# Value products one step later, and the key/value products split around the query products, in a two-layer cross-attention kernel

## The chip, the cores and the metric

One Trainium2 chip, one of its cores. The metric is the device time of one execution in microseconds (us), lower is better; the kernel before was timed three times, and its median is 1316.86 us (1316.17 to 1316.87).

## What is computed

Two layers of a gated cross-attention model on x (8 batches of 128 tokens, 512 wide) and a context of the same size:

```python
x = x + tanh(g_xattn[0]) * xattn0(layernorm(x), ctx, mask, ...)   # 32 query heads, 8 key/value heads, 128 wide
x = x + tanh(g_ffn[0])   * ffn0(layernorm(x), ...)                # gated, block-quantised weights and inputs
x = x + tanh(g_xattn[1]) * xattn1(layernorm(x), ctx, mask, ...)
x = x + tanh(g_ffn[1])   * ffn1(layernorm(x), ...)                # int4 weights, permuted inputs, bias
```

In an attention, q and k are normalised over each head (x * rsqrt(mean(x^2) + eps)), the softmax runs over 128 context positions in fp32, and four query heads share one key/value head.

## The kernel before, in words

**Units and steps.** A unit is one group (one key/value head with its four query heads) of one batch: 8 groups x 8 batches x 2 layers = 128 units. The kernel is a software pipeline of steps; step n works on four units at once. For unit n it makes keys and values (kv), queries (q), their normalisation and transposes; for unit n-1 the scores and the softmax; for unit n-2 the transposed probabilities and the value products; for unit n-3 the output products, which are added into x. Each engine has one function `step`, whose order of statements is the order of its queue; the engines meet only at semaphores.

**Products.** An fp32 product is made of three products of rounded halves (`hi` times `hi`, `hi` times `lo`, `lo` times `hi`), each over four k-tiles: `three_products` issues 12 matmuls, 512 wide for q and output, 256 wide for kv. The values take three matmuls. ScalarE (ACT) makes the `hi` half, VectorE (DVE) the `lo` half by subtraction. So `oT_hi`/`oT_lo` are halves of the attention output of unit n-3, both made from the PSUM bank `psPO`, and `pT_hi`/`pT_lo` those of the transposed probabilities.

**Steps 75 to 123.** Here (`by_dma`) the probabilities are not transposed on TensorE (PE). DVE writes them as two 16-bit planes (`probs_planes`), SyncE (SP) turns them with one DMA transpose (`turn_probs`), and DVE (`place_lower`, line 1027) and ACT (line 786) put the halves together in `p_whole`; ACT copies `pT_hi` from it (line 790) and DVE subtracts `pT_lo` (line 1032). In such a step PE's queue is: 12 kv, 12 q, 4 scores (8 records, as fp32 runs in two passes), 12 output, one transpose of k (`transposed_k`), 3 values, four transposes of q (`transposed_q`). `output()` waits for `o_lod`, the semaphore of `oT_lo`, ahead of its first product; `values()` waits for `pt_lod`, that of `pT_lo`; `transposed_k` waits for `kn_done`, the normalised keys.

**The other engines in such a step.** ACT: `oT_hi` (line 739), up to two or three pieces of weights rounded to `w_hi` (line 730), the square of k (748), `v_hi` (751), the four squares of q (769), `p_whole` and `pT_hi` (786, 790), the scaled `kn` (719), four exponentials (711), `qT` (836). DVE: inverse row sums, scaled probabilities, the planes, `oT_lo` (1085), `v_lo` (1102), `place_lower` (1027), masked scores (1138), maximum (1010), `pT_lo` (1032), scaled q (`qn`, 1040), `kT` (1164), the addition into x (1176). GpSimd (POOL): `w_lo` of the pieces (551), then the two small operations (576, 580) that turn the sums of squares into `rstd`, of which `kn` and `qn` are made.

**Around them.** Steps 0 to 47 are the first layer with the quantisation of feed-forward weights, steps 48 to 87 a written-out zone with the feed-forward of the first layer, steps 88 to 119 a loop of eight steps a turn (PE's own loop begins at step 80), and steps 120 on the last group and the second feed-forward. From step 124 on the probabilities are transposed on PE again.

Of the kernel before, what the change touches and what calls it, by code (L numbers as in the profile page):

```python
# [15 lines left out]
P = 128  # L16
# [80 lines left out]
def step_of(group, b):  # L97
# [6 lines left out]
              32: ((E + 1, 6), (E + 1, 7)), 33: ((E + 1, 8), (E + 1, 9), (E + 2, 0)), 34: ((E + 2, 1), (E + 2, 2)),  # L104
              35: ((E + 2, 3),), 36: ((E + 2, 4), (E + 2, 5)), 37: ((E + 2, 6),), 38: ((E + 2, 7), (E + 2, 8)),
# [51 lines left out]
def flamingo_kernel(nc, x, ctxT, mask, g_xattn, g_ffn, norms, wq, wkv, wo, ffn_w,  # L157
                    packedT, scalesT, perm, bias, w4_rows, out):
    top = ExitStack()
    with top:  # L160
# [211 lines left out]

        def turned_by_pe(n):

            return n - 1 - (DMA1 - DMA0 if isinstance(n, int) and n >= DMA1 else 0)
# [161 lines left out]
        def _(pool):  # L537
# [72 lines left out]
            def step(n, b, kind, j, q=None):  # L610
# [13 lines left out]
                if kind in (ZONE, PLAIN) and not calm(n, kind):  # L624
                    split_lower(split_pieces(n, b, kind, j))
# [46 lines left out]
        def _(act):  # L672
# [58 lines left out]

            def step(n, b, kind, j, q=None):
                t = Tiles(n, kind)
                exp_late = calm(n, kind) or (kind == FIRST and b == BATCHES - 1)
                if has(n, 3):

                    act.wait_ge(pv_ps, n - 2)
                    wait(act, y_ps, n - 3)
                    nc.scalar.activation(oT_hi[:, :], psPO[:, :], ACT.Copy).then_inc(o_hid, 1)
                if calm(n, kind) or (kind == ZONE and n == FFN0):  # L740
                    softmax_exp(n - 1)
                if kind in (ZONE, PLAIN) and not calm(n, kind):
                    split_upper(split_pieces(n, b, kind, j))
                if has(n, 0):

                    act.wait_ge(kv_ps, n + 1)
                    wait(act, rs_done, n)
                    nc.scalar.activation(kn[:, 0:P // 2].bitcast(BF16), kv_bank(n, kind)[:, 0:P], ACT.Square, scale=SCALE, accum_out=sumsq[:, REP:REP + 1])

                    wait(act, pv_ps, n - 3)  # L750
                    nc.scalar.activation(v_hi[:, b % 4, :], kv_bank(n, kind)[:, P:2 * P], ACT.Copy).then_inc(v_hid, 1)
                split_upper(late_pieces(n, kind))
# [12 lines left out]
                if has(n, 0):  # L765

                    act.wait_ge(q_ps, n + 1)
                    for h in range(REP):
                        last = nc.scalar.activation(squares[:, h // 2, (b + 1) % 4, h % 2, :], q_bank(n, kind)[:, h * P:(h + 1) * P], ACT.Square, scale=SCALE,  # L769
                                                    accum_out=sumsq[:, h:h + 1])  # L770
                    last.then_inc(sq_done, 1)
# [10 lines left out]
                if has(n, 2) and by_dma(n, kind):  # L782

                    act.wait_ge(pv_ps, n - 2)
                    act.wait_ge(planes_turned, (n - DMA0 + 1) * 16)
                    nc.scalar.activation(halves(p_whole[:, :])[:, :, 1], p_turned[:, 0:KT, :].rearrange("p k t -> p (k t)"),
                                         ACT.Copy).then_inc(upper_placed, 1)
                    act.wait_ge(upper_placed, n - DMA0 + 2)
                    act.wait_ge(lower_placed, n - DMA0 + 2)
                    nc.scalar.activation(pT_hi[:, :], p_whole[:, :], ACT.Copy).then_inc(pt_hid, 1)  # L790
# [36 lines left out]
                if has(n, 0):  # L827
# [8 lines left out]
                    nc.scalar.activation(qT[:, :], psSQ[:, :], ACT.Copy).then_inc(qT_sb, 1)  # L836
                if has(n, 1) and (t.next is not None or t.down is not None):
                    softmax_exp(n)
# [34 lines left out]
        def _(dve):  # L873
# [156 lines left out]
            def probs_lower(n, kind=None):  # L1030
                dve.wait_ge(pt_hid, n - 1)
                nc.vector.tensor_tensor(pT_lo[:, :], (p_whole if by_dma(n, kind) else psPO)[:, :], pT_hi[:, :].bitcast(FP32),
                                        ALU.subtract).then_inc(pt_lod, 1)
# [27 lines left out]
            def step(n, b, kind, j, q=None):  # L1061
# [5 lines left out]
                if has(n, 2):  # L1067

                    if not calm(n, kind):
                        row_inverse(n)  # L1070
                if by_dma(n, kind):
                    scaled_probs(n)
                    probs_planes(n)
                if q is not None and 0 < b <= QSTEPS:
# [7 lines left out]
                if has(n, 3):  # L1082

                    dve.wait_ge(o_hid, n - 2)
                    nc.vector.tensor_tensor(oT_lo[:, :], psPO[:, :], oT_hi[:, :].bitcast(FP32),
                                            ALU.subtract).then_inc(o_lod, 1)
# [3 lines left out]
                if t.last is not None:  # L1090
                    dve.wait_ge(x_acc, LAST0 + t.last + 1)
                    moments(NORM["last", t.last], t.last)
# [4 lines left out]
                if has(n, 2) and not t.active and not by_dma(n, kind):  # L1097
# [8 lines left out]
                if kind == ZONE and 0 <= n - INT4_0 < INT4_PARTS:  # L1106
                    int4_weights(n - INT4_0)
                for k in gathered(n, kind):

                    dve.wait_ge(wp_hid, k + 1)  # L1110
                    nc.vector.tensor_tensor(wp_lo[:, k, :], w4_turned[:, k, :], wp_hi[:, k, :].bitcast(FP32),
                                            ALU.subtract).then_inc(wp_lod, 1)
# [3 lines left out]
                if t.last is not None:  # L1116
                    wait(dve, xT_ps, 2 * BATCHES + t.last if t.last else 0)
                    normalise(NORM["last", t.last], t.last, f_s[:, :])
# [10 lines left out]
                if by_dma(n, kind):  # L1129
                    place_lower(n)  # L1130
# [12 lines left out]
                if by_dma(n, kind):  # L1143
                    probs_lower(n, kind)
                if has(n, 2) and (t.gate is not None or calm(n, kind)):
                    probs_lower(n, kind)
                if has(n, 0) and kind != FIRST and t.down is None:
                    scaled_q(n, kind, t)
                if has(n, 2) and qn_first(n, kind, t) and not calm(n, kind):
                    probs_lower(n, kind)  # L1150
# [4 lines left out]
                if has(n, 2) and t.gate is None and not qn_first(n, kind, t) and not by_dma(n, kind):  # L1155
                    probs_lower(n, kind)
# [13 lines left out]
                if has(n, 3):  # L1170
# [6 lines left out]
                                                   ALU.mult, ALU.add).then_inc(x_acc, 1)  # L1177
                if t.gate is not None:
# [107 lines left out]
        def _(pe):  # L1286
# [59 lines left out]
            def step(n, b, kind, j, q=None):  # L1346
# [22 lines left out]
                def output():  # L1369
                    pe.wait_ge(o_lod, n - 2)  # L1370
                    wait(pe, x_acc, n - 3)
                    if batch_of(n, 3, b) == 0:
                        pe.wait_ge(whole_w, group_of(n, 3, b, j) + 1)
                    three_products(psY[:, :], lambda a, h: (oT_hi, oT_lo)[a][:, h * P:(h + 1) * P],
                                   lambda a, h: weights(3, WO0 + h * D, D)[a]).then_inc(y_ps, 1)
# [13 lines left out]
                def values():  # L1389
                    pe.wait_ge(pt_lod, n - 1)  # L1390
                    if by_dma(n, kind):
                        pe.wait_ge(o_lod, n - 2)
                    slot = (b - 2) % 4
# [26 lines left out]
                if has(n, 0) and kind != FIRST:  # L1420
                    batch = batch_of(n, 0, b)

                    if kind != FIRST and batch == 0:
                        pe.wait_ge(qkv_split, group_of(n, 0, b, j))
                    wait(pe, kT_sb, n)
                    tok = slice(batch * P, (batch + 1) * P)
                    three_products(psKV[:, 0:2 * P], lambda a, k: (ctx_hi, ctx_lo)[a][:, batch, k * P:(k + 1) * P],
# [161 lines left out]
```

## Time and profile before

| what | value |
|---|---|
| median of three runs | 1316.86 us |
| the profiled execution | 1317.38 us, of it span 1315.6 us |
| PE busy | 1301.6 us, 99% |
| weight loads of PE (PEld) busy | 1102.0 us, 84% |
| DVE / ACT / POOL busy | 1002.2 / 866.9 / 621.4 us |
| granted TensorE clock | 1.000 over the whole span |
| HBM | 46 GB/s over the span |

The span runs from the first to the last instruction; the rest of the execution, 1.8 us, lies outside it. The ends of matmuls are modelled, so PE's busy share overstates its use: the distances between the starts of matmuls tell more than the share. Two layers of 128 steps fill the span, so one step of steps 75 to 123 takes about 9 us.

### The profile page before, as it was taken

What the parts mean: (1) busy time and instruction counts of PE and PEld (TensorE: products, weight loads), DVE (VectorE), ACT (ScalarE), POOL (GpSimd) and SP (SyncE); (2) the same over time, 40 slices, a digit from 0 to 9 for tenths busy, and PEclk for the clock granted to TensorE, in tenths of its full rate; (3) what the DMA queues carried; (4) which work ended last, traced back from release to release, by engine and by line L of the source; (5) the groups of instructions that cost most, each with busy time, mean ns of one, the idle gap of its engine ahead of it and who ended that gap; (6) DMA issues with size and microseconds to landing.
All of it is one profiled execution on the core that took longest, in us unless ns stands there. A gap on an engine that the chain in (4) does not pass through costs nothing.

```text
span 1315.6 us, 25535 instructions
## 1 busy us (share of the span) xinstructions
PE 1301.6 (99%) x7493; PEld 1102.0 (84%) x7493; DVE 1002.2 (76%) x2106; ACT 866.9 (66%) x3356; POOL 621.4 (47%) x683
## 2 busy tenths in 40 slices
PE   8999999999999999999999999999999999999999
PEld 7888888888888888877777788888888888888887
DVE  6878788787878788688888858777667677676756
ACT  5767667676767776645566456777767777676651
POOL 2546566565646566446677533532323323232232
PEclk9999999999999999999999999999999999999999
DMA  7011110111121011020301013623222122321001
GB/s 298 1 56 57 63 56 20 66 50 68 50 68 50 24 68 47 13 64 20 103 20 48 20 48 89 161 65 73 64 66 70 36 71 61 80 56 33 17 9 57
DMA packets 87338, 78.29 MB, mean 60 GB/s; under 512 B 70881, under 2 KB 75873, under 8 KB 83169
## 3 DMA queue, kind: packets, MB, share of 16 engines
q1 hardware_dynamic: 70272, 71.91, 18.6%
q10 hardware_dynamic: 16672, 4.46, 1.6%
q0 software_dynamic: 320, 1.05, 0.2%
q8 instruction: 33, 0.54, 0.2%
q14 instruction: 41, 0.33, 0.1%
HBM read 57.48 MB, written 3.15 MB: 46 GB/s over the span
## 4 chain that ended last, share of the span: by engine, by line
PE 84%; DVE 5%; issue 5%; DMA 2%; POOL 2%; ACT 1%; ACTq 0%; POOLq 0%; DVEq 0%; SPq 0%
PE bank L1298 60%; PE bank L1364 7%; PE bank L1290 7%; PE bank L1395 6%; PE bank L1326 2%; DMA p_turned<-p_planes 1%; PE bank L1381 1%; PE bank L1479 1%; POOL rstd L580 1%; DMA f_iqT<-f_iq 1%; DVE probs L1138 1%; ACT squares L769 0%; DMA ctx_raw<-in_ctxT 0%; DVE f_q L975 0%; DVE amax L968 0%
## 5 line engine op out<-in xcount | busy, mean ns | idle before, releaser
L551 POOL TENSOR_TENSOR w_lo<-w_raw,w_hi (+1 forms) x150 | 192.7, 1301 | 163.9 <-ACT w_hi L730 163.9
L769 ACT ACTIVATE squares<-bank 128x128 bf16<-128x128 f32 x512 | 134.4, 278 | 184.6 <-PE bank L1298 184.5
L711 ACT ACTIVATE probs<-probs,negmax 128x128 f32<-128x128 f32 x512 | 198.2, 391 | 7.0 <-DVE negmax L1010 4.5
L576 POOL TENSOR_TENSOR meansq<-sumsq,scalars 128x5 f32<-128x5 f32 x128 | 27.5, 215 | 352.5 <-ACT squares L769 352.5
L580 POOL TENSOR_TENSOR rstd<-meansq,scalars 128x5 f32<-128x5 f32 x128 | 152.9, 1194 | 10.7 <-POOL meansq L576 1.1
L1298 PE MATMUL bank<-w_hi,oT_hi 128*128 (+1 forms) x512 | 150.9, 416 | 0.0
L1298 PE MATMUL bank<-w_hi,xT_hi 128*128 (+1 forms) x512 | 140.1, 395 | 0.0
L1298 PE MATMUL bank<-w_lo,xT_hi 128*128 (+1 forms) x512 | 138.1, 390 | 0.3
L1364 PEld LDWEIGHTS bank<-kT,qT 128*128 128x128 f32 x1024 | 131.7, 191 | 7.7
L1298 PE MATMUL bank<-w_hi,oT_lo 128*128 (+1 forms) x512 | 138.0, 391 | 0.0
L1298 PE MATMUL bank<-w_lo,oT_hi 128*128 (+1 forms) x512 | 137.6, 390 | 0.0
L1298 PE MATMUL bank<-w_hi,xT_lo 128*128 (+1 forms) x512 | 136.9, 389 | 0.0
L1364 PE MATMUL bank<-kT,qT 128*128 128x128 f32 x1024 | 134.8, 274 | 0.0
L1138 DVE SCALAR_TENSOR_TENSOR probs<-bank,mask_sb 128x512 f32<-128x512 f32 x127 | 87.5, 689 | 58.3 <-PE bank L1364 40.5
L1298 PEld LDWEIGHTS bank<-w_lo,xT_hi 128*128 128x128 f32 x512 | 96.1, 188 | 22.7 <-DVE w_lo L904 1.4
L1298 PEld LDWEIGHTS bank<-w_lo,oT_hi 128*128 128x128 f32 x512 | 96.1, 188 | 21.6
L1298 PEld LDWEIGHTS bank<-w_hi,oT_lo 128*128 128x128 f32 x512 | 96.1, 188 | 21.2
L1298 PEld LDWEIGHTS bank<-w_hi,xT_lo 128*128 128x128 f32 x512 | 96.1, 188 | 19.9
L769 ACT ACTIVATION_READ_ACCUMULATOR squares<-bank 128x1 f32 x512 | 106.5, 208 | 0.0
L1298 PEld LDWEIGHTS bank<-w_hi,xT_hi 128*128 128x128 f32 x512 | 88.0, 189 | 11.8
L1298 PEld LDWEIGHTS bank<-w_hi,oT_hi 128*128 128x128 f32 x512 | 87.5, 189 | 12.4
L711 ACT ACTIVATION_READ_ACCUMULATOR probs<-probs,negmax 128x1 f32 x512 | 96.9, 189 | 0.0
(129 smaller groups left out, 3000.2 us busy)
## 6 DMA issues: line engine op xcount, KB each, us to landing
w_raw<-in_wq SPq DMA_DIRECT2D x16, 1024.0 KB, 4.8
w_raw<-in_wo SPq DMA_DIRECT2D x16, 1024.0 KB, 9.6
w_raw<-in_wkv SPq DMA_DIRECT2D x16, 512.0 KB, 5.6
fw_raw<-in_ffn_w SPq DMA_DIRECT2D x36, 192.0 KB, 2.3
x_sb<-in_x SPq DMA_DIRECT2D x7, 256.0 KB, 10.4
ctx_raw<-in_ctxT SPq DMA_DIRECT2D x7, 256.0 KB, 9.8
fw_raw<-in_ffn_w SPq DMA_DIRECT2D x7, 256.0 KB, 2.6
out<-x_sb SPq DMA_DIRECT2D x7, 256.0 KB, 2.0
```

The costliest lines, as they stand in the source:

```text
L551: last = nc.gpsimd.tensor_tensor(lo, raw, hi.bitcast(FP32), ALU.subtract)
L576: nc.gpsimd.tensor_tensor(meansq[:, :], sumsq[:, :], eps_sb[:, :], ALU.add).then_inc(ms_done, 1)
L580: nc.gpsimd.tensor_tensor(rstd[:, :], meansq[:, :], minus_half[:, :], ALU.pow).then_inc(rs_done, 1)
L711: last = nc.scalar.activation(probs[:, h * P:(h + 1) * P], probs[:, h * P:(h + 1) * P], ACT.Exp, bias=negmax[:, h:h + 1], accum_out=rowsum ...
L769: last = nc.scalar.activation(squares[:, h // 2, (b + 1) % 4, h % 2, :], q_bank(n, kind)[:, h * P:(h + 1) * P], ACT.Square, scale=SCALE, a ...
L1138: nc.vector.scalar_tensor_tensor(heads(probs[:, :]), heads(psSQ[:, :]), SCALE, mask_sb[:, :].unsqueeze(1).to_broadcast([P, REP, P]), ALU.m ...
L1290: last = nc.tensor.transpose(dst[:, k * P:(k + 1) * P], src[:, k * P:(k + 1) * P], m)
L1298: last = nc.tensor.matmul(dst, left(a, k), right(b, k), start=(n == 0), stop=(n == len(terms) - 1))
L1326: last = nc.tensor.matmul(ps[:, 0:width], f_xqT[:, k, :], wT[:, col:col + width], start=(k == 0), stop=(k == KT - 1))
L1364: last = nc.tensor.matmul(psSQ[:, h * P:(h + 1) * P], qT[:, h * P:(h + 1) * P], kT[:, :], start=True, stop=True)
L1381: nc.tensor.transpose(kv_bank(n, kind)[:, 2 * P:3 * P], kn[:, :], ident[:, :]).then_inc(kt_ps, 1)
L1395: last = nc.tensor.matmul(psPO[:, :], v[:, slot, :], p[:, :], start=(k == 0), stop=(k == 2))
```

## The change

It concerns steps 76 to 124 (`values_late`), all but the first of the steps with a DMA transpose and the one behind them.

- PE: four of the 12 kv products, then the 12 q products, then the three value products of unit n-3 (one step later than before), then the other eight kv products, scores, the first eight output products, the transpose of k, the last four output products, the four transposes of q.
- ACT: the squares of q come first (their unused output goes to `qn`'s memory), then `oT_hi`, then the square of k (which now signals `sq_done`), `v_hi`, the pieces of `w_hi`; the halves `p_whole` and `pT_hi` move to the end of the step, behind `qT`, also in step 75.
- DVE: `pT_lo` of the step before stands between the scaled probabilities and the planes, `oT_lo` behind the planes, `place_lower` at the end of the step.
- POOL: `rstd` comes ahead of the step's `w_lo`.
- The pieces of weights in steps 81 to 83 are dealt out two a step; one-off work of the zone is moved on DVE; in step 124 the moments and the normalisation of the first batch of the second feed-forward come earlier on DVE.

```diff
+        def values_late(n, kind):
+            return kind == PLAIN or (isinstance(n, int) and DMA0 < n <= DMA1)
@@ POOL
-                if kind in (ZONE, PLAIN) and not calm(n, kind):
+                if kind in (ZONE, PLAIN) and not calm(n, kind) and not values_late(n, kind):
                     split_lower(split_pieces(n, b, kind, j))
...
+                if values_late(n, kind):
+                    split_lower(split_pieces(n, b, kind, j))
@@ ACT
+            def q_squares(n, b, kind):
+                act.wait_ge(q_ps, n + 1)
+                for h in range(REP):
+                    dump = (qn[:, h * P // 2:(h + 1) * P // 2].bitcast(BF16) if values_late(n, kind)
+                            else squares[:, h // 2, (b + 1) % 4, h % 2, :])
+                    last = nc.scalar.activation(dump, q_bank(n, kind)[:, h * P:(h + 1) * P], ACT.Square, scale=SCALE,
+                                                accum_out=sumsq[:, h:h + 1])
+                return last
+            def output_upper(n):
+                act.wait_ge(pv_ps, n - 2)
+                wait(act, y_ps, n - 3)
+                nc.scalar.activation(oT_hi[:, :], psPO[:, :], ACT.Copy).then_inc(o_hid, 1)
...
                 if has(n, 0):
+                    if values_late(n, kind):
+                        q_squares(n, b, kind)
+                        output_upper(n)
                     act.wait_ge(kv_ps, n + 1)
...
+                if values_late(n, kind):
+                    split_upper(split_pieces(n, b, kind, j))
...
+                if has(n, 2) and by_dma(n, kind):
+                    if not values_late(n, kind):
+                        act.wait_ge(pv_ps, n - 2)
+                    act.wait_ge(planes_turned, (n - DMA0 + 1) * 16)
+                    nc.scalar.activation(halves(p_whole[:, :])[:, :, 1], ...).then_inc(upper_placed, 1)
+                    act.wait_ge(upper_placed, n - DMA0 + 2)
+                    act.wait_ge(lower_placed, n - DMA0 + 2)
+                    nc.scalar.activation(pT_hi[:, :], p_whole[:, :], ACT.Copy).then_inc(pt_hid, 1)
@@ DVE
+            def whole_lower(n):
+                dve.wait_ge(pt_hid, n - 2)
+                nc.vector.tensor_tensor(pT_lo[:, :], p_whole[:, :], pT_hi[:, :].bitcast(FP32),
+                                        ALU.subtract).then_inc(pt_lod, 1)
...
+                if by_dma(n, kind) or t.last == 0:
+                    scaled_probs(n)
+                if values_late(n, kind):
+                    whole_lower(n)
                 if by_dma(n, kind):
-                    scaled_probs(n)
                     probs_planes(n)
...
+                if values_late(n, kind):
+                    output_lower(n)
...
+                if by_dma(n, kind):
+                    place_lower(n)
@@ PE
-                    three_products(psY[:, :], ...).then_inc(y_ps, 1)
+                    for part in (slice(0, 2 * KT), slice(2 * KT, 3 * KT)):
+                        last = three_products(psY[:, :], ..., part)
+                        if values_late(n, kind) and has(n, 0) and part.start == 0:
+                            transposed_k()
+                    last.then_inc(y_ps, 1)
...
+                    if values_late(n, kind):
+                        wait(pe, kT_sb, n)
+                        keys_values(slice(0, KT))
+                        queries()
+                        values(3)
+                        keys_values(slice(KT, 3 * KT)).then_inc(kv_ps, 1)
```

## Rows read from the trace of the kernel before

**Rows 1.** Timeline, PE, one step: start us, us, engine, line, operation, count.
```profile
1018.28 0.72 PE L1298 MATMUL bank<-w_hi,ctx_hi 128*128 x4
1018.84 0.64 PE L1298 MATMUL bank<-w_lo,ctx_hi 128*128 x4
...
1019.80 1.09 PE L1298 MATMUL bank<-w_hi,xT_hi 128*128 x4
...
1022.55 1.05 PE L1364 MATMUL bank<-kT,qT 128*128 128x128 f32 x8
1023.36 1.17 PE L1298 MATMUL bank<-w_hi,oT_hi 128*128 x4
...
1026.18 0.28 PE L1381 MATMUL bank<-ident,kn 128*128 128x128 f32 x1
1026.21 0.48 PE L1395 MATMUL bank<-pT_hi,v_hi 128*128 128x512 f32 x1
...
1027.35 0.71 PE L1298 MATMUL bank<-w_hi,ctx_hi 128*128 x4
```

**Rows 2.** Timeline, PE, the scores of steps 75, 76, 123 and 124.
```profile
790.32 1.05 PE L1364 MATMUL bank<-kT,qT 128*128 128x128 f32 x8
...
800.60 1.05 PE L1364 MATMUL bank<-kT,qT 128*128 128x128 f32 x8
...
1231.05 1.05 PE L1364 MATMUL bank<-kT,qT 128*128 128x128 f32 x8
...
1241.65 0.61 PE L1364 MATMUL bank<-kT,qT 128*128 128x128 f32 x4
```

**Rows 3.** Waits of weight loads, 789 to 1232 us: total us, times, longest.
```profile
PEld bank L1381 <- ACT kn L719: 4.3, 5, 1.5
```

**Rows 4.** Timeline, the longest wait: DMA transpose issued, and its reader.
```profile
835.50 1.23 SPq L486 DMA_TRANSPOSE p_turned<-p_planes  x1
...
841.05 0.78 ACT L786 ACTIVATE p_whole<-p_turned 128x512 uint16<-128x512 uint16 x1 [1.82 <-DMA p_turned<-p_planes]
```

**Rows 5.** Timeline, the other engines in the step of rows 1.
```profile
1018.62 0.60 ACT L836 ACTIVATE qT<-bank 128x512 f32<-128x512 f32 x1 [0.34 <-PE bank L1290]
...
1019.12 0.59 ACT L739 ACTIVATE oT_hi<-bank 128x512 fp32r<-128x512 f32 x1
...
1019.96 0.68 DVE L1085 TENSOR_TENSOR oT_lo<-bank,oT_hi 128x512 fp32r<-128x512 f32 x1
...
1020.15 1.23 SPq L486 DMA_TRANSPOSE p_turned<-p_planes  x1
...
1022.75 0.28 ACT L769 ACTIVATE squares<-bank 128x128 bf16<-128x128 f32 x1 [1.58 <-PE bank L1298]
...
1023.20 0.46 DVE L1027 COPY p_whole<-p_turned 128x512 uint16<-128x512 uint16 x1 [1.70 <-DMA p_turned<-p_planes]
...
1023.76 0.80 ACT L786 ACTIVATE p_whole<-p_turned 128x512 uint16<-128x512 uint16 x1
...
1024.24 1.17 POOL L580 TENSOR_TENSOR rstd<-meansq,scalars 128x5 f32<-128x5 f32 x1
...
1024.59 0.63 ACT L790 ACTIVATE pT_hi<-p_whole 128x512 fp32r<-128x512 f32 x1
...
1025.25 0.69 DVE L1032 TENSOR_TENSOR pT_lo<-p_whole,pT_hi 128x512 fp32r<-128x512 f32 x1 [0.20 <-ACT pT_hi L790]
1025.44 0.37 ACT L719 ACTIVATE kn<-bank,rstd 128x128 f32<-128x128 f32 x1 [0.22 <-POOL rstd L580]
```

**Rows 6.** Timeline, a weight load that waited for DVE.
```profile
762.72 0.68 DVE L1032 TENSOR_TENSOR pT_lo<-bank,pT_hi 128x512 fp32r<-128x512 f32 x1
...
763.45 0.19 PEld L1395 LDWEIGHTS bank<-pT_hi,v_hi 128*128 128x128 f32 x1
```

**Rows 7.** Timeline, DVE beside POOL's `w_lo` in one step.
```profile
807.41 2.72 POOL L551 TENSOR_TENSOR w_lo<-w_raw,w_hi 128x512 fp32r<-128x512 f32 x2 [3.96 <-ACT w_hi L730]
...
808.91 1.51 DVE L1052 TENSOR_SCALAR nibble_i<-packed_sb 128x512 int32<-128x512 int32 x1
```

More of the change, by code:

```diff
@@ L764, in step @@
                     hidden_turned(0, t.down)
[L765 to L771, printed above, removed]
+                if has(n, 0) and not values_late(n, kind):
+                    q_squares(n, b, kind).then_inc(sq_done, 1)
                 if t.first is not None:
@@ L1028, in place_lower, with last_normalised, output_lower, probs_lower @@
                                       ).then_inc(lower_placed, 1)
-            def probs_lower(n, kind=None):
+            def last_normalised(i):
+                wait(dve, xT_ps, 2 * BATCHES + i if i else 0)
+                normalise(NORM["last", i], i, f_s[:, :])
+            def whole_lower(n):
+                dve.wait_ge(pt_hid, n - 2)
+                nc.vector.tensor_tensor(pT_lo[:, :], p_whole[:, :], pT_hi[:, :].bitcast(FP32),
+                                        ALU.subtract).then_inc(pt_lod, 1)
+            def output_lower(n):
+                dve.wait_ge(o_hid, n - 2)
+                nc.vector.tensor_tensor(oT_lo[:, :], psPO[:, :], oT_hi[:, :].bitcast(FP32),
+                                        ALU.subtract).then_inc(o_lod, 1)
+            def probs_lower(n):
                 dve.wait_ge(pt_hid, n - 1)
-                nc.vector.tensor_tensor(pT_lo[:, :], (p_whole if by_dma(n, kind) else psPO)[:, :], pT_hi[:, :].bitcast(FP32),
+                nc.vector.tensor_tensor(pT_lo[:, :], psPO[:, :], pT_hi[:, :].bitcast(FP32),
                                         ALU.subtract).then_inc(pt_lod, 1)
@@ L1081, in step @@
                     nc.vector.scalar_tensor_tensor(xb, psC[:, :], down_gate[:, :], xb, ALU.mult, ALU.add).then_inc(d_acc, 1)
[L1082 to L1086, printed above, removed]
+                if has(n, 3) and not values_late(n, kind):
+                    output_lower(n)
                 if t.acc is not None:
@@ L1096, in step @@
                     row_inverse(n)
-                if has(n, 2) and not t.active and not by_dma(n, kind):
+                if has(n, 2) and not t.active and not by_dma(n, kind) and t.last != 0:
                     scaled_probs(n)
@@ L1105, in step @@
                         ctx_lower(t.first)
-                if kind == ZONE and 0 <= n - INT4_0 < INT4_PARTS:
+                if kind == ZONE and 0 <= n - INT4_0 < INT4_PARTS and not values_late(n, kind):
                     int4_weights(n - INT4_0)
[L1108 to L1112, printed above, removed]
                 if t.first is not None:
@@ L1115, in step @@
                     normalise(t.first, t.first, f_s[:, :])
-                if t.last is not None:
-                    wait(dve, xT_ps, 2 * BATCHES + t.last if t.last else 0)
-                    normalise(NORM["last", t.last], t.last, f_s[:, :])
+                if t.last is not None and t.last:
+                    last_normalised(t.last)
                 if t.norm is not None:
@@ L1461, in step @@
                     output()
[L1462 to L1467 removed]
+                if has(n, 0):
+                    if not values_late(n, kind):
+                        transposed_k()
                     transposed_q()
```

104 lines of the change are left out of this document (52 added, 52 removed).

## The prediction

> **What bounds the kernel now.** I read three views of the stretch that the change touches. The timeline of PE comes first [rows 1]: in one step the starts of its matmuls follow each other without a hole, from the first kv product at 1018.28 to that of the next step at 1027.35, 9.06 us. The scores start at 800.60 in step 76 and, 47 steps on, at 1231.05 in step 123 [rows 2]: 430.45 us, or 9.16 us a step. 47 steps of 9.06 are 425.8 us, so only 4.7 us of the stretch are waits; the step ahead of it (790.32 to 800.60) took 10.28, 1.2 too much. The list of waits says what for: the transpose of k on PE waited for ACT's `kn` five times, 4.3 us in all [rows 3]. Last, the timeline round the longest of these: the DMA transpose was issued at 835.50, ACT could read it at 841.05 [rows 4], 5.5 us instead of the usual 3.05 (1020.15 to 1023.20, [rows 5]); `kn` stands behind `p_whole` in ACT's queue. So PE's own work bounds the stretch, with about 5.5 us of waits on late DMA transposes, 0.4% of the span, as all that there is to win. That some of the 4.7 are loop edges (about 0.1 each, five of them) I estimate from what the waits leave over.
>
> **What a step costs PE after the change.** No matmul is added or removed: 12 kv, 12 q, 8 score records, 12 output, one k transpose, three values, four q transposes. An fp32 matmul ahead of a 512-wide product costs a changeover: the four first output products take 1.00 where a product otherwise takes 0.23 (0.92) [rows 1]. Before there are such changes behind the scores, behind k's transpose and behind q's; after, k's transpose is followed by an output product instead of a value product, so their number is the same. I allow 0.01 us a step for the second start of the kv products.
>
> **Where PE stands in a new step,** in us from its first kv product, with no waits: q from 0.56 (a third of the kv: 1018.28 to 1018.84), values from 3.31 (q takes 2.75, 1019.80 to 1022.55), kv again from 4.00 (3 x 0.23), scores from 4.96 (8 x 0.12, as 1018.84 to 1019.80), the last score record 5.73, output from 5.76, k's transpose about 7.68, the end 9.06 [rows 1]. Against that stand three chains, each made of [rows 5, 6]:
>
> *Values.* Before, the values waited in the same step for a transpose that had just landed. Now their chain starts at the end of the last step: `qT` starts at 0.34 (1018.62), `p_whole` 0.50 later (as 1019.12 stands behind 1018.62), `pT_hi` 0.83 later, which ends 0.63 later at 2.30, `pT_lo` ends at 2.33 + 0.69 = 3.02, and the weight load may go 0.05 later: in [rows 6] DVE ended at 763.40 and the load began at 763.45. That is 3.07; PE wants it one product ahead of 3.31, at 3.08. Not a wait, by 0.01 us; without the four early kv products it would be 0.5.
>
> *Keys.* k's square starts when kv is done, about 0.32 behind the start of its last product at 4.84, so 5.16. Each of the four squares of q held ACT for 0.25 (1022.75 to 1023.76), and POOL's `rstd` was done 1.65 after the last of them (1024.24 + 1.17 = 1025.41) [rows 5]; for k that makes 5.41 and 7.06. `kn` starts 0.03 later and takes 0.37, 7.45, load 7.50. PE wants it at 7.45: 0.05 late, if nothing else delays PE. That `w_lo` comes after `rstd` and `p_whole` after `qT` takes both out of this chain; two pieces of `w_hi` fit on ACT between `v_hi` (about 5.7) and 7.08.
>
> *Output.* Here I find a new wait. The squares of q start 0.43 behind the start of the last q product (3.08 + 0.43 = 3.51; before, 1022.75 against 1022.32). They keep ACT for 1.01 (until 1023.76), and `oT_hi` is now behind them: 4.52, its end 0.59 later 5.11, `oT_lo` 0.03 later for 0.68, 5.83, and the load of the first output product 5.88, since `output()` waits for `oT_lo` before anything. PE wants that load when the last score record starts, at 5.73. Before, `oT_lo` was done at 1020.64, 2.7 us ahead of the need; now it is 0.15 late in every step. All lengths are of the same instructions in the same shapes, and the values themselves (done at 4.19) come before 4.52, so ACT's order decides, not the values. This wait also covers the keys' 0.05: the chains don't add.
>
> The Trainium skill ("TensorE: Matmul & The Clock Gate", Part 1, on the gap between matmuls) gives N / 2.4 GHz + 2.5 ns from start to start, an estimate of 0.216 us for a 512-wide product; the rows show 0.23, and I use them. By the page's figure PE's cover between the last q product and the last score record would be 2.5 instead of 2.65 us and the wait near 0.28, some 6 us more over the stretch.
>
> DVE has room: eight operations 512 wide at about 0.7 [rows 5] and a few shorter ones make 6.9 us of a step, and `place_lower`, now last, starts at about 9.7 and ends before 1.1 of the next step. The DMA transpose is issued at about 3.8 and lands at 6.9; it is needed at 9.7, and even the worst landing (5.5 us, [rows 4]) makes 9.3. So the waits of [rows 3] go altogether; what takes their place is the wait for `oT_lo`. If the transposes were still too slow, half of the old waits would stay, 2.7 us.
>
> **The edges.** Step 75 loses its values (0.69) and its wait for the DMA; scores of 75 to scores of 76: 4.1 + 4.96 = 9.05 against 10.28 [rows 2], gain 1.2. Step 124 has both the late values and its own. From scores to scores it took 1241.65 - 1231.05 = 10.60 [rows 2]. After: 4.3 left of step 123, scores no earlier than 5.88 plus four transposes of the probabilities (0.11 each), because these go into the bank that `oT_lo` empties at 5.83: 10.6. The earlier normalisation on DVE saves a wait there, this one takes it back: 0, give or take 0.4.
>
> **The sum.** Waits that go: 1.2 + 4.7 - 0.55 of loop edges = 5.4. Waits that come: 47 x (0.15 + 0.01) = 7.5 us; bounds of this term 47 x 0.01 = 0.5 (no wait at all) and 47 x 0.25 = 11.8 (one more handover of 0.05 and 0.05 for a value or k transpose that comes late too). In three steps `wp_hi` delays `kn` by under 0.1, nothing. Net +2.1, and I take off 0.3 for rounding the wait up (it is 0.146 with unrounded starts): +1.8. The profiled execution would go from 1317.38 (span 1315.6 and 1.8 around it) to 1319.2; it lies 0.5 above the median of the runs, so the median would be 1318.7.
>
> **The rivals.** What this kernel's runs can tell from no change is about 0.2%, 2.6 us.
>
> *Faster: the output wait is hidden.* If ACT's four squares overlap more than before, or the load can go before `oT_lo`, only the keys' 0.05 remains, or nothing: -5.4 + 47 x 0.06 = -2.6, or down to -4.9: 1311.9 to 1314.3. For it: the miss is 0.15 in a chain of 2.8. Against it: each length in [rows 5] is that of an instruction that doesn't change. Chance 0.17.
>
> *Slower: POOL's `w_lo` holds up DVE.* DVE operations on SBUF alone stretch beside `w_lo`: the one at 808.91 took 1.51 us, twice a 512-wide one, and ended just behind the `w_lo` that ran until 810.13 [rows 7]. Now `w_lo` (2.72 for two pieces) runs from about 7.1 to 9.8 in steps with two pieces, right ahead of `place_lower`. If it ends later than about 0.8 in the next step, `place_lower`, the scaled probabilities and `pT_lo` are late and the values wait. The price: one held operation, up to 0.6 us, less the 0.15 that is lost anyway, in some 30 steps with two pieces: +13 on the forecast, about 1332. Against it: by the rows it ends 0.6 into the next step or sooner. Chance 0.1.
>
> *Slower: the new waits are as said but a little longer* (0.2 to 0.25, ACT or DVE handing over later, a chain that adds after all), +4 to +6.5 on before: 1321 to 1323.4. Chance 0.18.
>
> *The DMA waits stay in part,* because load and transpose collide at another place: +4.5, 1321.4. Chance 0.06.
>
> *My forecast,* 1316.3 to 1319.5: 0.49.
>
> From these: faster by over 0.2% 0.17; within 0.2% 0.49; slower 0.34. The range from 1313.8 to 1323.0 leaves out the deeper part of the fast case and the POOL case.
>
> **What the profile would show.** Right: steps of 9.21 us from 76 to 123; in each a wait of about 0.15 us of the first output product's weight load for DVE's `oT_lo`; none of k's transpose for `kn`, or under 0.05; no wait of PE that goes back to a DMA transpose. Wrong if the steps take 9.06 to 9.12 (then the output chain is shorter), if the value products wait for `pT_lo`, or if `place_lower` takes about 1 us.

## The result, and the profile after

The change makes the kernel slower: 1323.54 us (median of five runs, 1323.43 to 1323.86) against 1316.51 us (five runs, 1315.90 to 1316.87), a ratio of 1.0053 with the interval [1.0042, 1.0063], or 7.0 us. The forecast was 1318.7 with a range up to 1323.0, so the sign of the net was right, its size was not, and the time lies 0.5 us above the range. The profiled execution took 1323.74 us, its span 1321.9, at a granted clock of 0.999.

The page's line of busy times tells little. PE's busy time is 7.6 us more than before with the same 7493 weight loads (16 records of matmuls are missing after), so a longer "busy" here is no new work: the drawn lengths of matmuls overlap, and starts that are pushed apart fill more of the span.

```profile
span 1321.9 us, 25454 instructions
...
PE 1309.2 (99%) x7477; PEld 1107.1 (84%) x7493; DVE 997.6 (75%) x2106; ACT 876.6 (66%) x3356; POOL 618.0 (47%) x683
```

The timeline of PE for one new step (start, us, engine, line, operation, count), to be held against [rows 1]:

```profile
1019.03 0.72 PE L1338 MATMUL bank<-w_hi,ctx_hi 128*128 x4
1019.59 1.09 PE L1338 MATMUL bank<-w_hi,xT_hi 128*128 x4
...
1022.34 0.39 PE L1439 MATMUL bank<-pT_hi,v_hi 128*128 128x512 f32 x1
...
1023.02 0.64 PE L1338 MATMUL bank<-w_lo,ctx_hi 128*128 x4
...
1024.95 1.20 PE L1338 MATMUL bank<-w_hi,oT_hi 128*128 x4
...
1026.90 0.27 PE L1425 MATMUL bank<-ident,kn 128*128 128x128 f32 x1
1026.93 1.17 PE L1338 MATMUL bank<-w_hi,oT_lo 128*128 x4
...
1028.29 0.48 PE L1338 MATMUL bank<-w_hi,ctx_hi 128*128 x2
```

In us from the first kv product: q at 0.56, values at 3.31, kv again at 3.99, output at 5.92, k's transpose at 7.87, the end at 9.26. The prediction had 0.56, 3.31, 4.00 and then 5.76 + 0.15 = 5.91. Up to the output products the step runs as it was drawn.

Where the scores start in steps 75, 76, 123 and 124, the answers to [rows 2]:

```profile
791.08 1.05 PE L1404 MATMUL bank<-kT,qT 128*128 128x128 f32 x8
...
800.39 0.83 PE L1404 MATMUL bank<-kT,qT 128*128 128x128 f32 x6
...
1237.41 0.83 PE L1404 MATMUL bank<-kT,qT 128*128 128x128 f32 x6
...
1248.20 1.06 PE L1404 MATMUL bank<-kT,qT 128*128 128x128 f32 x8
```

| stretch, scores to scores | before | after | forecast |
|---|---|---|---|
| start of the span to step 75 | 790.32 | 791.08 | as before |
| step 75 to 76 | 10.28 | 9.31 | 9.05 |
| step 76 to 123 (47 steps) | 430.45 | 437.02 | 433.5 |
| step 123 to 124 | 10.60 | 10.79 | 10.6 |
| step 124 to 125 | 10.16 | 9.97 | as before |

The rows of the table give +6.3 us, as the spans do (1315.6 to 1321.9). The first, 0.8, lies ahead of the changed steps, and over the profiles of all kernels of this study it lay between 789.75 and 791.08; it is no effect of the change that I can name. Of the forecast's miss, 4.5 us for the profiled execution (1319.2 foreseen, 1323.74 found), 3.5 us lie in the 47 steps. They come in three kinds, read from the starts of the scores:

- 36 intervals of 9.23 to 9.29, nearly all 9.25, where 9.21 was forecast and 9.06 is PE's own work;
- ten of 9.37 to 9.42, two in eight steps;
- one of 9.84, from step 79 to step 80.

**The wait that the list doesn't show.** A reader who goes to the list of waits of weight loads first, as one would, finds no `oT_lo` there. These are its only two lines for 789 to 1240 us (total us, times, longest), in place of the 4.3 us for `kn` of [rows 3]:

```profile
PEld bank L1338 <- issue: 3.2, 11, 0.5
PEld bank L1338 <- DVE kT L1202: 0.2, 1, 0.2
```

The list counts idle time between the records of loads. The load ahead of this one starts 0.30 us before it instead of 0.11, but is drawn 0.19 us long; 0.11 us of idle time are left (1024.84 to 1024.95), and idle times that short have no line in the list. In the ten steps of 9.4 the idle time is 0.25 to 0.28 us and is listed, but put down to "issue": ten of the eleven of its first line are this wait (2.7 of the 3.2 us), and the eleventh, 0.5 us, is that of step 80. One of the ten:

```profile
1015.71 0.31 PEld L1338 LDWEIGHTS bank<-w_hi,oT_hi 128*128 128x128 f32 x2 [0.28 <-issue]
```

The starts show it in every step. Here is PEld, where the load of the first output product starts at 1024.95, and DVE, whose `oT_lo` starts at 1024.20 for 0.69, hence ends at 1024.89:

```profile
1024.20 0.64 PEld L1404 LDWEIGHTS bank<-kT,qT 128*128 128x128 f32 x5
1024.95 0.53 PEld L1338 LDWEIGHTS bank<-w_hi,oT_hi 128*128 128x128 f32 x3
...
1024.20 0.69 DVE L1064 TENSOR_TENSOR oT_lo<-bank,oT_hi 128x512 fp32r<-128x512 f32 x1 [1.49 <-ACT oT_hi L751]
```

What it costs is read from start to start. The medians of the steps between 1000 and 1180 us are, in ns, the whole step from scores to scores:

| | last score record to first output product | first to second output product | whole step |
|---|---|---|---|
| before | 31 | 314 | 9054 |
| after | 195 | 337 | 9254 |

The first two differences, 164 and 23, are 187 of the 200 ns by which the step has grown; the other 13 are spread over many products by a few ns each. The second start of the kv products, for which 0.01 us was allowed, cost nothing: the twelve take 1.51 us from start to start in both kernels. ACT's rows say why the load is late, four squares and then `oT_hi`, at 4.53 of the step (4.52 was forecast):

```profile
1022.54 0.28 ACT L743 ACTIVATE qn<-bank 128x128 bf16<-128x128 f32 x1 [1.23 <-PE bank L1338]
...
1023.56 0.61 ACT L751 ACTIVATE oT_hi<-bank 128x512 fp32r<-128x512 f32 x1
1024.17 0.28 ACT L769 ACTIVATE kn<-bank 128x128 bf16<-128x128 f32 x1
```

No wait of PE goes back to a DMA transpose any longer, in none of the 48 steps, though one of these still landed 4.65 us after its issue.

**Step 79 to 80.** POOL's `w_lo` now comes behind `rstd`, and the first kv products of a new group need it:

```profile
829.08 1.20 POOL L584 TENSOR_TENSOR rstd<-meansq,scalars 128x5 f32<-128x5 f32 x1
830.27 2.52 POOL L555 TENSOR_TENSOR w_lo<-w_raw,w_hi 128x512 fp32r<-128x512 f32 x2
...
832.99 0.78 PE L1338 MATMUL bank<-w_hi,ctx_hi 128*128 x4 [0.28 <-POOL w_lo L555]
```

Step 79 makes the last two pieces of the group that step 80 begins with. Before, they were done ahead of `rstd`, at 829.1; now at 832.8, when PE is already there. In the later turns three steps lie between the last of these pieces and its first use, and the wait doesn't occur.

### The profile page after: what moved, and what is told of

It reads as the page before. It is cut to its first block, busy times and chain, and to the rows that moved or that the text cites. A ratio compares the mean times of both kernels' runs of the same rounds, so it can differ in the third digit from the quotient of the medians.

```text
span 1321.9 us, 25454 instructions
## 1 busy us (share of the span) xinstructions
PE 1309.2 (99%) x7477; PEld 1107.1 (84%) x7493; DVE 997.6 (75%) x2106; ACT 876.6 (66%) x3356; POOL 618.0 (47%) x683
## 4 chain that ended last, share of the span: by engine, by line
PE 88%; issue 4%; DVE 3%; POOL 3%; DMA 1%; ACT 1%; POOLq 0%; ACTq 0%; DVEq 0%
PE bank L1338 63%; PE bank L1404 8%; PE bank L1330 7%; PE bank L1439 6%; PE bank L1366 2%; PE bank L1425 1%; POOL rstd L584 1%; POOL w_lo L555 1%; PE bank L1534 1%; DMA f_iqT<-f_iq 0%; DMA ctx_raw<-in_ctxT 0%; DVE f_q L996 0%; DVE amax L989 0%; POOL probs L621 0%; DVE bank L1020 0%
## 5 line engine op out<-in xcount | busy, mean ns | idle before, releaser
L743 ACT ACTIVATE squares<-bank 128x128 bf16<-128x128 f32 x316 | 83.3, 279 | 93.4 <-PE bank L1338 93.3
L1338 PE MATMUL bank<-w_hi,oT_lo 128*128 (+1 forms) x512 | 142.7, 400 | 0.0
L1064 DVE TENSOR_TENSOR oT_lo<-bank,oT_hi 128x512 fp32r<-128x512 f32 x125 | 84.2, 674 | 75.9 <-ACT oT_hi L751 75.9
L1404 PEld LDWEIGHTS bank<-kT,qT 128*128 128x128 f32 x1024 | 128.6, 191 | 4.0
L1214 DVE SCALAR_TENSOR_TENSOR x_sb<-bank,scalars,x_sb 128x512 f32<-128x512 f32 x125 | 93.6, 749 | 32.1 <-PE bank L1338 28.0
L1338 PEld LDWEIGHTS bank<-w_hi,oT_lo 128*128 128x128 f32 x512 | 92.4, 188 | 22.1
L725 ACT ACTIVATE kn<-bank,rstd 128x128 f32<-128x128 f32 x128 | 47.1, 368 | 81.3 <-POOL rstd L584 81.3
```

The costliest lines, as they stand in the source:

```text
L725: nc.scalar.activation(kn[:, :], kv_bank(n, kind)[:, 0:P], ACT.Copy, scale=rstd[:, REP:REP + 1]).then_inc(kn_done, 1)
L743: last = nc.scalar.activation(dump, q_bank(n, kind)[:, h * P:(h + 1) * P], ACT.Square, scale=SCALE, accum_out=sumsq[:, h:h + 1])
L1214: nc.vector.scalar_tensor_tensor(xb, psY[:, :], tanh_gates[:, layer:layer + 1], xb, ALU.mult, ALU.add).then_inc(x_acc, 1)
L1338: last = nc.tensor.matmul(dst, left(a, k), right(b, k), start=(n == 0), stop=(n == len(terms) - 1))
L1404: last = nc.tensor.matmul(psSQ[:, h * P:(h + 1) * P], qT[:, h * P:(h + 1) * P], kT[:, :], start=True, stop=True)
```

## The experiments

Two theories stood against each other. *Output*: the 0.19 us of a step are the wait of the first output product for `oT_lo`, which is late because ACT makes `oT_hi` behind four squares. *Reorder*: PE itself loses the time on its new order (a second start of the kv products, k's transpose between output products), whatever ACT does. In the results, "step" is the commonest distance from scores to scores, and "47 steps" that from step 76 to 123.

**Experiment 1: the wait for `oT_lo` only ahead of the four products that read it.**

```diff
                 def output():
-                    pe.wait_ge(o_lod, n - 2)
+                    pe.wait_ge(o_hid if values_late(n, kind) else o_lod, n - 2)
...
                             transposed_k()
+                        if values_late(n, kind) and part.start == 0:
+                            pe.wait_ge(o_lod, n - 2)
```

> PE waits for oT_hi ahead of the output products and for oT_lo only ahead of the last four. Theory (the new cost is the wait for oT_lo ahead of the first output product, 0.19 us a step, and what PE's sequencer does exposed behind it): the wait goes, a wait of 0.04 for the scaled keys comes, steps of 9.10 us instead of 9.25, 1315 to 1317 us in all, against 1323.5. Rival A (splitting the kv products costs PE itself): steps stay at 9.25, 1323. Rival B (the wait moves on to the transpose of k): steps of 9.2, 1321.

Measured: 1313.55 us (nine runs, 1312.45 to 1314.53) beside 1316.45 (18 runs) of the kernel before, ratio 0.9978 [0.9968, 0.9988]. Step 9.09, 47 steps 427.74. The output products now start while DVE is still at `oT_lo`:

```profile
1018.40 1.06 PE L1404 MATMUL bank<-kT,qT 128*128 128x128 f32 x8
...
1019.21 1.17 PE L1338 MATMUL bank<-w_hi,oT_hi 128*128 x4
...
1018.62 0.69 DVE L1064 TENSOR_TENSOR oT_lo<-bank,oT_hi 128x512 fp32r<-128x512 f32 x1 [1.49 <-ACT oT_hi L751]
```

Nothing of PE's order was changed and 9.3 us of the 47 steps went, so *reorder* falls as the cause of the 0.19; at most the 0.03 us by which 9.09 still exceeds the 9.06 of before is left to it. From the last score record to the first output product are 31 ns again, and 314 to the second. The 0.02 us by which 9.09 exceeds the 9.07 of experiment 2 are spread over some output products at 231 to 237 ns in place of 227, and why is open. The ten intervals of 9.4 went too. The time is 1.5 us under the lowest that was expected: the expectation multiplied 0.15 us by the steps and left out the ten intervals (1.5 us), and 0.7 us lies ahead of step 75 (790.35 against 791.08), where nothing was changed.

**Experiment 2: `oT_hi` ahead of the last of the four squares.** The same wait is attacked from the other side: PE waits as in the changed kernel, ACT is earlier.

```diff
                 for h in range(REP):
+                    if values_late(n, kind) and h == REP - 1:
+                        output_upper(n)
...
                         q_squares(n, b, kind)
-                        output_upper(n)
```

> ACT makes oT_hi after three of q's four squares instead of after all four. Theory: oT_hi starts 0.25 us sooner, at 4.27 (the values are done at 4.19), oT_lo is done at 5.6, before PE wants it at 5.72; the fourth square still ends before kv is done, so rstd comes no later: steps of 9.10, 1315 to 1317 us. Rival A (PE's own order): 9.25, 1323. Rival B (keys late): the fourth square pushes the square of k, kn comes 0.2 later, steps of 9.25 with another wait.

Measured: 1313.81 us (ten runs, 1313.01 to 1314.26), ratio 0.9979 [0.9969, 0.9989]. Step 9.07, two in eight 9.12 to 9.18, 47 steps 427.74. This too is under the expected 1315 to 1317. A square costs ACT 0.25, more than the 0.19 that were missing; moving one is worth 9.3 us over the stretch. `oT_lo` ends at 1019.23 and the output starts at 1019.38:

```profile
1018.54 0.69 DVE L1065 TENSOR_TENSOR oT_lo<-bank,oT_hi 128x512 fp32r<-128x512 f32 x1 [1.24 <-ACT oT_hi L753]
...
1018.57 1.06 PE L1405 MATMUL bank<-kT,qT 128*128 128x128 f32 x8
1019.38 1.17 PE L1339 MATMUL bank<-w_hi,oT_hi 128*128 x4
```

So two edits that share nothing but this wait give back the same time.

**Experiments 3 and 4: none, or eight, of the twelve kv products ahead of q.** The split moves work between the two chains: ahead of q it covers the values, behind the values it covers the output.

```diff
-                        keys_values(slice(0, KT))
+                        # 3: no line here; 4: keys_values(slice(0, 2 * KT))
                         queries()
                         values(3)
-                        keys_values(slice(KT, 3 * KT)).then_inc(kv_ps, 1)
+                        # 3: keys_values().then_inc(kv_ps, 1); 4: keys_values(slice(2 * KT, 3 * KT)).then_inc(kv_ps, 1)
```

> All 12 kv products behind the values, none ahead of q. Theory: the values are wanted at 2.52 but pT_lo is there at 3.07: PE waits 0.55 us there, no wait for oT_lo; steps of 9.6, 1340 us. Rival (the values' chain has room and only the output wait counts): steps of 9.06, 1315 us.

> Eight of the 12 kv products ahead of q. Theory: q ends 0.48 us later in the step while the output is wanted at the same place, so the wait for oT_lo grows from 0.19 to 0.67: steps of 9.73, 1346 us. Rival (the values' chain is what costs): more cover for it, steps shorter than 9.25, under 1323 us.

Measured with none: 1329.03 us (one run), step 9.43, 47 steps 443.81. The wait shows in the list, total, times and longest, and in the rows of one step, DVE ending at 1014.46 and the load at 1014.51:

```profile
PEld bank L1439 <- DVE pT_lo L1058: 20.2, 42, 0.5
...
1013.77 0.69 DVE L1058 TENSOR_TENSOR pT_lo<-p_whole,pT_hi 128x512 fp32r<-128x512 f32 x1 [0.56 <-ACT pT_hi L857]
...
1014.51 0.19 PEld L1439 LDWEIGHTS bank<-pT_hi,v_hi 128*128 128x128 f32 x1 [0.48 <-DVE pT_lo L1058]
```

Measured with eight: 1346.80 us (one run), step 9.73, 47 steps 459.74. Moving four more products of 0.12 ahead takes 0.48 from the output's cover, and the step grows by 9.73 - 9.25 = 0.48:

```profile
1006.25 0.69 DVE L1064 TENSOR_TENSOR oT_lo<-bank,oT_hi 128x512 fp32r<-128x512 f32 x1 [1.97 <-ACT oT_hi L751]
...
1007.00 0.50 PE L1338 MATMUL bank<-w_hi,oT_hi 128*128 x1 [0.40 <-DVE oT_lo L1064]
```

What follows: the third ahead of q is needed for the values, and the output's lateness goes one to one into the step (the load 0.19 late in the changed kernel and the step 0.20 longer than before, 0.67 late here and 0.68 longer). The values' lateness doesn't, and so the 9.6 and 1340 us expected of none were too long. In that kernel the values' load starts 0.67 us behind the load ahead of it instead of 0.23, so 0.44 late, and 9.43 is only 0.37 above 9.06. Behind a 512-wide product some 0.1 us of lateness thus cost nothing. Why is argued, not shown: there a load usually starts 0.22 us ahead of its own product, in a row of 256-wide products 0.12 us ahead, and that is enough.

**Experiment 5: the last pieces of step 80's weights a step earlier.**

```diff
-30: ((E + 1, 2), (E + 1, 3)), 31: ((E + 1, 4), (E + 1, 5)),
+30: ((E + 1, 2), (E + 1, 3), (E + 1, 4)), 31: ((E + 1, 5),),
```

> The last kv piece of the group that starts at step 80 gets its w_lo one place earlier: three pieces in step 78, one in step 79. Theory (POOL makes w_lo behind rstd, so the second piece of step 79 ends 0.4 us into step 80, whose first kv product needs it): the wait of PE's load there goes, the interval of 9.84 us between scores becomes 9.25, the whole 0.6 us less, 1322.9. Rival (the third piece pushes POOL and ACT in step 78): as much comes back there, no difference.

Measured: 1322.88 us (one run), 47 steps 436.54, 0.5 less than the changed kernel. The interval of 9.84 became 9.11, but the one ahead of it went from 9.26 to 9.47. There POOL now has three pieces, and `place_lower` on DVE lasts three times its usual 0.46:

```profile
823.36 1.37 DVE L1048 COPY p_whole<-p_turned 128x512 uint16<-128x512 uint16 x1
```

The cause of the 9.84 is shown, since moving `w_lo` moves the wait (the line of 0.5 us under "issue" is gone too), and the prediction's POOL rival appears, in one step, as soon as `w_lo` has three pieces.

**Experiments 6 and 9: what the intervals of 9.4 wait for.** In such a step the first output product comes 1.16 us behind the first score record (1014.56 to 1015.72), not 0.98. Two ideas: the second semaphore wait, for a new group's weights, and its register arithmetic come too late (experiment 6 puts it ahead of the one for `oT_lo`), or PE's sequencer works out the weights' address only once `oT_lo` has been seen (experiment 9 asks for that address ahead of the waits).

```diff
# 6
-                    pe.wait_ge(o_lod, n - 2)
-                    wait(pe, x_acc, n - 3)
                     if batch_of(n, 3, b) == 0:
                         pe.wait_ge(whole_w, group_of(n, 3, b, j) + 1)
+                    pe.wait_ge(o_lod, n - 2)
+                    wait(pe, x_acc, n - 3)
# 9, beside the lines of 6; the products' weights are then w_hi[:, bass.ds(first + h * D, D)]
+                    first = WO0 + (group_of(n, 3, b, j) % 2) * WSLOT
+                    if not isinstance(first, int):
+                        first = pe.snap(first)
```

> In output() the wait for whole_w, with its register arithmetic, stands ahead of the wait for oT_lo instead of behind it. Theory (PE's sequencer is held at oT_lo and does the arithmetic only afterwards, while PE is idle): the steps that take 9.41 us, one in eight, become 9.25, some 6 of them, 1 us in all, 1322.5. Rival (those steps are longer for the weights' own sake): they stay at 9.41.

> The address of the output weights is put in a register ahead of the waits of output(), the wait for whole_w too; moving the latter alone changed nothing. Theory (what was left behind the wait is the arithmetic for the weights' addresses): the steps of 9.41 us become 9.25 to 9.3, about 1 us in all, 1322.5. Rival (the arithmetic is done again for each product): they stay at 9.4, 1323.2.

Measured: 1323.15 us with these steps at 9.39 and 9.40 (experiment 6), and 1323.16 us with them at 9.39 to 9.43 (experiment 9), one run each. The first idea is at most 0.03 us: the operation of line 1413 is gone from behind the wait in both, and there the load comes 0.195 us behind the end of `oT_lo` instead of 0.226. The second wasn't put to the test by its edit: the trace still has the register operation of the product's line ahead of the load. The sequencer's records of the changed kernel in a step of 9.41 are, start us and ns:

```
1015.521  32 ALU_OP       L1413
1015.613  46 FUSED_REGOPS L1338
1015.708 186 LDWEIGHTS    L1338 bank<-w_hi,oT_hi
```

In a step of 9.25 no register operation stands between the last score's load and that of the output, and the load comes 0.05 us behind the end of `oT_lo`; in each of the ten long steps one or two stand there, and it comes 0.21 or 0.23 us behind. In experiment 1 the same FUSED_REGOPS stands in the same place in the same steps, PE isn't held there, and the output starts 31 ns behind the last score record as in every step. So I take the extra 0.16 us for address arithmetic that usually runs ahead of the engine and lies bare when the queue is held up right before it. No run removed the arithmetic alone, and so this stays argued, not shown.

**Experiment 8: `oT_hi` ahead of all four squares.**

```diff
-                        q_squares(n, b, kind)
                         output_upper(n)
+                        q_squares(n, b, kind)
```

> ACT makes oT_hi ahead of all four squares of q. Theory: oT_hi starts when the values are done, 4.2 us into the step, oT_lo is in time, but the squares end 0.55 us later and rstd and kn with them: PE waits at the transpose of k instead, kn there at 8.0 against 7.4 wanted, of which 0.1 is free: steps of 9.5 us, 1335 us. Rival (the keys have room): 9.07, 1314.

Measured: 1333.57 us (one run), steps 9.47 to 9.59 but for the one at step 80 (10.37), 47 steps 447.67, as the theory had it. What the output gains, the keys lose, since `rstd` waits for the squares:

```profile
PEld bank L1425 <- ACT kn L725: 29.7, 46, 0.7
```

With `oT_hi` behind four squares the output's load is 0.19 late; ahead of all four the load of k's transpose is 0.60 late, of which 0.43 is in the step; behind three both are nearly free.

**Experiments 7 and 10: the repairs together.** 7 is the edits of 1, 2 and 5; 10 is those of 2, 5 and 9.

> Both edits that shorten the output wait (oT_hi after three squares, oT_lo waited for ahead of the last four products), and the piece of step 79. Theory: each alone already hides the wait; together they take the last 0.03 us a step and the register arithmetic, and 0.7 us at step 80: steps of 9.06, 1312.0 to 1313.0 us, 0.27 to 0.33% under before. Rival (the keys' chain is what is left): 9.09 a step, no better than either alone, 1313.5.

> oT_hi after three squares, the piece of step 79, and the register of the output weights ahead of the waits; oT_lo is waited for ahead of all output products as in the changed kernel. Theory: steps of 9.06 us without the 0.1 more that one step in four has with the ACT edit alone, 0.5 us less than the two edits that were run together: 1312.3, 0.3% under before. Rival: the arithmetic stays behind the wait, 1313.3.

Measured: 7 took 1312.79 us (nine runs, 1312.56 to 1313.46) beside 1316.12 (13 runs), ratio 0.9974 [0.9965, 0.9984], step 9.09, 47 steps 427.41; its scores of steps 76 and 123:

```profile
800.17 1.06 PE L1405 MATMUL bank<-kT,qT 128*128 128x128 f32 x8
...
1227.58 0.61 PE L1405 MATMUL bank<-kT,qT 128*128 128x128 f32 x4
```

10 took 1313.62 us (11 runs, 1312.97 to 1314.22) beside 1316.30 (15 runs), ratio 0.9981 [0.9972, 0.9990], 47 steps 427.72. The wait is paid for once, so 1 and 2 don't add. Of 7 the time came out as its theory had it, but not the step: 9.09 is what its rival had. Of 10 the rival was right: its steps are 9.05 to 9.09 and two in eight 9.11 to 9.15 (9.12 to 9.18 in experiment 2), so the register asked for ahead of the waits took at most 0.03 us off those. Version 7 has the lowest median and beats both kernels, the one before by 3.3 us and the changed one by more than 10; between it and 1, 2 or 10 the intervals don't decide. In its step with three pieces POOL holds `place_lower`, and the values wait half a microsecond, once:

```profile
820.45 3.78 POOL L555 TENSOR_TENSOR w_lo<-w_raw,w_hi 128x512 fp32r<-128x512 f32 x3
...
823.00 1.56 DVE L1049 COPY p_whole<-p_turned 128x512 uint16<-128x512 uint16 x1
...
826.06 0.19 PEld L1445 LDWEIGHTS bank<-pT_hi,v_hi 128*128 128x128 f32 x1 [0.54 <-DVE pT_lo L1059]
```

## Why the prediction was wrong

**The step that failed** is the term of the sum "waits that come: 47 x (0.15 + 0.01) = 7.5 us". Its mechanism was right and its size was not, and two waits that belong to the change were put at nothing: the stretch took 437.02 us where 425.8 + 0.55 + 7.5, less 0.3, makes 433.5. The 3.5 us are these.

- *The wait itself, 2.0 us.* 9.25 instead of 9.21, 0.04 in each of 47 steps. `oT_hi` took 0.61 where 0.59 was put in, `oT_lo` 0.69 where 0.68 was, the load came at 5.92 instead of 5.88, which makes it 0.19 late and not 0.15, and the second output product was another 0.02 later. I had taken 0.3 off the term for rounding; the rounding went the other way. A wait of 0.15 that is the difference of two chains of 2.8 us has the errors of both.
- *Ten longer steps, by my reading address arithmetic, 1.0 us.* Ten intervals are 0.11 to 0.17 longer and three beside them 0.03, 1.5 us in all, of which the 0.55 allowed for loop edges covered a third. That a wait at the end of a queue also bares what the sequencer does behind it was in no step of mine.
- *`w_lo` at step 80, 0.6 us.* I followed `w_lo` behind `rstd` to DVE, and not to PE, which reads it. The reader a step later was the one that waited.

**The range.** The wait measured, 9.3 us over the stretch with its address arithmetic (437.02 less the 427.74 of experiment 1), lies within the term's bounds of 0.5 and 11.8. The end of the range, 1323.0, is about what the term's upper bound alone gives (1316.9 + 6.4), and so had no room for anything else: the 0.6 us of step 80, 0.3 at step 75 to 76 and the 0.8 us ahead of step 75 came on top. The last is no effect that I can name, and without it the profiled execution would lie inside the range, so that the time fell on this side of its end is in part chance. The rival "a little longer" (1321 to 1323.4, chance 0.18) comes nearest, but it isn't quite what happened: the wait was 0.19 and not 0.2 to 0.25, and the rest of the time came from what it doesn't name.

**The values** were right: `pT_lo` was done at 3.00 (3.02 forecast) and they started at 3.31 (3.31). That they would be 0.5 late without the early kv products was 0.44 for the load and 0.37 for the step (experiment 3): I had counted the whole lateness of the load as lost time, and behind a 512-wide product it isn't.

**The keys** never showed in the changed kernel, as their 0.05 was covered by the output's wait: `kn` was done at 7.42 of the step (7.45 forecast), 0.21 ahead of the load that needs it. In experiments 1 and 2, where the output wait is gone, that load goes 0.05 behind the end of `kn`, so the keys do hold it, but it starts only 0.03 later than usual and the transpose at most 0.004. So the 0.05 was a true reading of the chain and no cost.

**The waits that go** went as forecast: 1.0 us at step 75 to 76 (1.2 forecast; there the first kv product's load now waited 0.2 for DVE's `kT`, the second line of the list of waits), and none on a transpose after. **Step 124** cost 10.79 to the 10.6 forecast, and the next interval gave the 0.2 back.

**The rivals.** "The output wait is hidden" was false of the changed kernel and is true of experiments 1, 2, 7 and 10; it gave 1311.9 to 1314.3, and they took 1312.8 to 1313.8. "POOL holds up DVE" was false with two pieces a step: `place_lower` took 0.46, starting at 1028.80, 0.2 us behind the end of `w_lo`, which began at 1026.03 and ran 2.54.

```profile
1026.03 2.54 POOL L555 TENSOR_TENSOR w_lo<-w_raw,w_hi  x2
...
1028.80 0.46 DVE L1048 COPY p_whole<-p_turned 128x512 uint16<-128x512 uint16 x1
```

With three pieces it is true (1.37 and 1.56 us, experiments 5 and 7): there `place_lower` began 0.23 and 0.05 us into the third piece, which lasts 1.28, and both times it ended 0.32 us behind that piece. The prediction's "DVE operations on SBUF alone" is too wide, though: `negmax`, which reads and writes SBUF alone, began beside a `w_lo` 130 times in the twelve profiles of this study and never took more than its usual 0.69 us. The Trainium skill ("SBUF — State Buffer", section "SBUF: two separate sides") says that DVE and GpSimd share one pair of ports, which an instruction that needs it holds until its end while the other blocks; on DVE these are only instructions in a mode that uses two ports, or with two inputs from SBUF. The rows agree with it in the main, though a copy that waited for the whole piece should end 0.46 us behind it and not 0.32; no run here tells which mode a DVE instruction was in.

The matmul pitch of the Trainium skill ("TensorE: Matmul & The Clock Gate", Part 1, on the gap between matmuls), by which the prediction's alternative came out some 6 us longer, at about 1324.7, is nearer to the measured time than my sum, but not for its reason: the twelve q products took 2.75 us (1019.59 to 1022.34), 0.229 each, as before. The page's 0.216 isn't what this trace shows.

## What to carry to other kernels

When a chain is moved to make room for another, list for every engine what now stands ahead of each *old* consumer: here a slack of 2.7 us for `oT_lo` became a debt of 0.19 through four short squares, and moving one of them back turned 7 us lost into 2.6 us won. Put a semaphore wait ahead of the first instruction that reads the data, not ahead of the group: products of `oT_hi` needn't wait for `oT_lo`. When a wait is the small difference of two long chains, plan with a range for it: 0.01 to 0.02 in each of a few lengths made 0.15 into 0.19 here. And a producer whose place in a queue moves is to be followed to all of its readers, those of the next step too.

## What the runs showed of the hardware that I had not expected

- A wait of 0.16 us, 0.19 with what follows it, in each of 47 steps, over 8 us, is in the list of waits under its own name in none: the record of the load ahead (0.19 us) leaves only 0.11 us idle, which isn't listed, and in the ten longer steps it stands under "issue". Only the distance from start to start shows it.
- Behind a 512-wide product the first part of a weight load's lateness cost nothing (0.44 late cost 0.37, 0.60 late cost 0.43, 0.03 late at most 0.004), while behind a 128-wide fp32 product lateness counted in full (0.19 late, 0.20 longer; 0.67 and 0.68).
- Where PE's queue was held at a semaphore and a register operation stood between it and the load, the load came 0.21 to 0.23 us behind the releasing instruction instead of 0.05; where the queue wasn't held (experiment 1), the same operation cost nothing. That the operation is the cause is argued.
- The same `COPY` of 128 x 512 on DVE took 0.46 us behind POOL's `w_lo` and 1.37 to 1.56 us beside it, while `negmax` on DVE was never longer beside it.
- The same two instructions, `oT_hi` on ACT and `oT_lo` on DVE, took 0.61 and 0.69 us instead of the 0.59 and 0.68 of [rows 5]; why is open.
